# Where the second bias of the edge messages is added, who splits the messages, and what the store and the row loads wait for

## The reference

```python
h = jnp.maximum(_layernorm(x, axis=-1), 0.0)
msg_input = jnp.concatenate([h[src], h[dst]], axis=1)
for t in range(4):
    m = jax.nn.relu(msg_input @ W1[t] + b1[t]) @ W2[t] + b2[t]
    msgs = msgs + jnp.where((edge_type == t)[:, None], m, 0)
agg = jax.ops.segment_sum(msgs, dst, num_segments=num_nodes)
gi = agg @ W_ih.T + b_ih
gh = h @ W_hh.T + b_hh
r = sigmoid(i_r + h_r); z = sigmoid(i_z + h_z); n = tanh(i_n + r * h_n)
out = x + (1 - z) * n + z * h
```

## Time and profile before

| | |
|---|---|
| runs | 1735.42, 1740.06 and 1738.05 us, median 1738.05 us |
| the profiled execution, its own time | 1735.05 us |
| its span in the profile | 1733.2 us |
| mean granted clock of TensorE | 0.978 of the higher level |
| busy: PE, PEld | 1616.9 us (93%), 1421.4 us (82%) |
| busy: DVE, ACT, POOL | 1629.0 us (94%), 1458.7 us (84%), 1003.4 us (58%) |
| chain that ended last, PE's share | PE bank lines 1% each and less, mixed with DVE and ACT lines |

### The profile page before, as it was taken

The page is one execution under the profiler, slowest core; times in us unless marked ns, Lnnn a source line. Parts: engine busy times, 40 slices in busy tenths (PEclk is TensorE's granted clock), DMA queues, the critical chain, the costliest instruction groups (busy, mean ns, idle before and its releaser), DMA issues. The chain is left out here.

```text
span 1733.2 us, 43005 instructions
## 1 busy us (share of the span) xinstructions
PE 1616.9 (93%) x10182; PEld 1421.4 (82%) x10182; DVE 1629.0 (94%) x4752; ACT 1458.7 (84%) x3404; POOL 1003.4 (58%) x1325
## 2 busy tenths in 40 slices
PE   0337999999999999999999999999999999999998
PEld 0326888888888888888888888888888888888887
DVE  8987999999999999999999999999999999999986
ACT  0126999999999999999999999999999999999896
POOL 5755656666666666655555555565655555555500
PEclk9956999999999999999999999999999999999999
DMA  2235777777777777777777777777777777777653
GB/s 84 70 87 154 193 195 206 203 200 200 203 200 203 199 199 203 198 200 196 199 198 200 200 195 201 196 200 195 197 201 194 201 196 199 197 196 200 188 143 100
DMA packets 477080, 320.07 MB, mean 185 GB/s; under 512 B 105917, under 2 KB 463117, under 8 KB 476974
## 3 DMA queue, kind: packets, MB, share of 16 engines
q10 hardware_dynamic: 261792, 156.12, 29.3%
q1 hardware_dynamic: 186638, 107.42, 25.5%
q0 software_dynamic: 28544, 55.41, 13.1%
HBM read 212.08 MB, written 107.07 MB: 184 GB/s over the span
## 5 line engine op out<-in xcount | busy, mean ns | idle before, releaser
L613 POOL DMA_INDIRECT e_x<-in_x,rows_now x816 | 824.4, 1010 | 248.4 <-issue 239.0
L1258 ACT ACTIVATE e_h<-e_x,shift,rstd 128x128 f32<-128x128 f32 x816 | 355.8, 486 | 90.0 <-DVE shift L1114 57.0
L1275 ACT ACTIVATE n_h<-n_x,shift,rstd 128x128 f32<-128x128 f32 x784 | 385.3, 492 | 2.9 <-issue 2.9
L1414 PE MATMUL bank<-n_h_hi,whh_hi 128*128 128x512 f32 x588 | 249.2, 424 | 1.2 <-ACT n_zc L1366 1.2
L1414 PE MATMUL bank<-n_a_hi,wih_hi 128*128 128x512 f32 x588 | 246.4, 419 | 0.9 <-DVE bank L1154 0.9
L1494 PE MATMUL bank<-n_sel,n_win 128*128 128x256 f32 x1568 | 234.7, 292 | 0.4 <-DVE n_sel L1142 0.4
L1416 PE MATMUL bank<-n_a_hi,wih_lo 128*128 128x512 f32 x588 | 232.5, 395 | 0.0
L1416 PE MATMUL bank<-n_h_hi,whh_lo 128*128 128x512 f32 x588 | 231.7, 394 | 0.0
L1415 PE MATMUL bank<-n_h_lo,whh_hi 128*128 128x512 f32 x588 | 231.2, 393 | 0.0
L1142 DVE TENSOR_SCALAR n_sel<-iota,n_rel 128x256 fp32r<-128x256 f32 x784 | 229.6, 357 | 0.1
L1415 PE MATMUL bank<-n_a_lo,wih_hi 128*128 128x512 f32 x588 | 229.6, 391 | 0.0
(11 more groups left out here) (193 smaller groups left out, 3812.4 us busy)
## 6 DMA issues: line engine op xcount, KB each, us to landing
n_win<-messages SPq DMA_DIRECT2D x1568, 64.2 KB
messages<-e_msg ACTq DMA_DIRECT2D x204, 257.0 KB, 2.9
n_x<-in_x ACTq DMA_DIRECT2D x195, 256.0 KB
out<-n_out ACTq DMA_DIRECT2D x195, 256.0 KB
e_x<-in_x,rows_now POOLq DMA_INDIRECT x816
rows_now<-lists SPq DMA_DIRECT2D x204, 2.0 KB
lists<-picks,list_rows POOLq DMA_INDIRECT x54, 2.8
w<-in_W SPq DMA_DIRECT2D x1, 512.0 KB, 5.0
```

The costliest lines, as they stand in the source:

```text
L613: G.indirect_dma_start(e_x[:, s, 2 * end + t, :], None, x, bass.IndirectOffsetOnAxis(ap=rows_now[:, s, t, end:end + 1], axis=0)).then_inc( ...
L1258: last = A.activation(e_h[:, s % 2, k, :], e_x[:, s, k, :], ACT.Relu, scale=rstd[:, slot, col + k:col + k + 1], bias=shift[:, slot, col + ...
L1275: last = A.activation(n_h[:, s % 2, cols], n_x[:, s, cols], ACT.Relu, scale=rstd[:, slot, col + 4 + k:col + 5 + k], bias=shift[:, slot, co ...
L1414: T.matmul(o, w_hi, v_hi, start=start, stop=False, skip_group_check=onto)
```

## The change

1. The bias product on TensorE is gone; the W2 products start the accumulation themselves. b2, spread over all partitions, keeps a tile of its own, b2_two.
2. DVE gets `biased` at the end of its step q + 9: bank BE1 plus b2_two, written as full-precision numbers into the low half's place in e_msg (semaphore e_biased). W1 of the next unit waits for that instead of e_low.
3. e_high copies from there, in SBUF, instead of the bank, in ACT's step q + 10 behind the first pair of normalise_edges and ahead of n_r.
4. `low_half` is gone from DVE; POOL subtracts in SBUF, low = low - high, behind the second pair of gathers and ahead of `write_half`.
5. store_messages stands behind the second pair of normalise_edges; in the head at the end of ACT's step.
6. SP loads the windows by pairs of types. In even steps the loads of types 0 and 1 wait for the store of unit g + 4 and those of types 2 and 3 for unit g + 5; odd steps wait for no store.

```diff
@@ SP, window loads @@
-                    if isinstance(g, int):
-                        for q in range(0 if g == 0 else min(g + AHEAD, UNITS), min(g + AHEAD + 1, UNITS)):
-                            sp.wait_ge(e_stored[q % UNROLL], uses(q, q % UNROLL, UNROLL, 16))
-                    else:
-                        q, qs = g + AHEAD, (m - LAG + 2 + AHEAD) % UNROLL
-                        sp.wait_ge(e_stored[qs], uses(q, qs, UNROLL, 16))
...
+                    for pair_ in range(2):
+                        if m % 2 == 0:
+                            q = g + AHEAD - 1 + pair_
...
+                        for half in range(2):
+                            for t in (2 * pair_, 2 * pair_ + 1):
...
@@ POOL @@
+            def low_half(i, m):
+                q, s = i - 10, (m - 10) % UNROLL
+                if within(q, UNITS):
+                    pool.wait_ge(e_high, q + 1)
+                    G.tensor_tensor(e_msg[:, s, :, D:2 * D], e_msg[:, s, :, D:2 * D].bitcast(F32),
+                                    e_msg[:, s, :, 0:D].bitcast(F32), ALU.subtract).then_inc(e_low, 1)
...
                 if within(i, UNITS):
                     gather(i, m, (1,))
+                low_half(i, m)
                 if h is not None:
                     write_half(h)
@@ DVE @@
-                in_head = isinstance(i, int) and i < LAG - 2
-                if not in_head:
-                    low_half(i, m)
                 ln_part(i, m, 0)
...
+                biased(i, m)
                 if isinstance(i, int) and i == GENERAL_STEP:
                     general_sums()
+
+            def biased(i, m):
+                q, s = i - 9, (m - 9) % UNROLL
+                if within(q, UNITS):
+                    dve.wait_ge(e_messaged, q + 1)
+                    first = 2 * ((m - 9) % 2)
+                    V.tensor_tensor(e_msg[:, s, :, D:2 * D].bitcast(F32),
+                                    bank[BE1][:, message_part].rearrange("p (t d) -> p t d", t=2),
+                                    b2_two[:, first * D:(first + 2) * D].rearrange("p (t d) -> p t d", t=2),
+                                    ALU.add).then_inc(e_biased, 1)
@@ ACT @@
                 normalise_edges(i, m, (0, 1))
+                q, s = i - 10, (m - 10) % UNROLL
+                if within(q, UNITS):
+                    act.wait_ge(e_biased, q + 1)
+                    act.wait_ge(e_tagged, q + 1)
+                    A.activation(e_msg[:, s, :, 0:D], e_msg[:, s, :, D:2 * D].bitcast(F32), ACT.Copy).then_inc(e_high, 1)
...
-                store_messages(i, m)
                 normalise_edges(i, m, (2, 3))
+                in_head = isinstance(i, int) and i < LAG - 2
+                if not in_head:
+                    store_messages(i, m)
@@ PE @@
-                        pe.wait_ge(e_low, q)
+                        pe.wait_ge(e_biased, q)
...
-                    T.matmul(bank[BE1][:, message_part], ones_r[:], b2_rows[:, first * D:(first + 2) * D],
-                             start=True, stop=False)
                     for t in range(2):
                         o = bank[BE1][:, 2 * P + t * D:2 * P + (t + 1) * D]
-                        last = T.matmul(o, e_r[:, s, t * P:(t + 1) * P], w2[:, first + t, :], start=False, stop=t == 1)
+                        last = T.matmul(o, e_r[:, s, t * P:(t + 1) * P], w2[:, first + t, :], start=True, stop=True)
```

More of the change, by code:

```diff
@@ L144, in gnn_layer @@
         b2_rows = sb("b2_rows", [P, TYPES * D], F32R)
+        b2_two = sb("b2_two", [P, TYPES * D])
         row_is = sb("row_is", [P, 2])
@@ L235, in gnn_layer @@
         descends = borrow(n_zc[:], 0, ECOLS)
-        b2_two, b2_hi, b2_lo, b2_parts = (
-            e_msg[:].rearrange("p r t w -> p (r t w)")[:, at * TYPES * D:(at + 1) * TYPES * D] for at in range(4))
-        b2_two, b2_parts = b2_two.bitcast(F32), b2_parts.bitcast(F32)
+        b2_hi, b2_lo, b2_parts = (
+            e_msg[:].rearrange("p r t w -> p (r t w)")[:, at * TYPES * D:(at + 1) * TYPES * D] for at in range(3))
+        b2_parts = b2_parts.bitcast(F32)
         ends = n_d[:].rearrange("p r w -> p (r w)").bitcast(I32).rearrange("p (k e c) -> p k e c", k=SEGMENTS, e=2)
@@ L390, in gnn_layer @@
         e_high = sem("e_high")
+        e_biased = sem("e_biased")
         e_low = sem("e_low")
@@ L557, in step @@
                     if isinstance(g, int) and due(g - 3):
                         sp.wait_ge(n_summed, g - 3)
[L559 to L566, removed]
+                    for pair_ in range(2):
+                        if m % 2 == 0:
+                            q = g + AHEAD - 1 + pair_
+                            if not isinstance(g, int):
+                                qs = (m - LAG + 2 + AHEAD - 1 + pair_) % UNROLL
+                                sp.wait_ge(e_stored[qs], uses(q, qs, UNROLL, 16))
+                            else:
+                                for stored in range(pair_ if g == 0 else q, min(q + 1, UNITS), 2):
+                                    sp.wait_ge(e_stored[stored % UNROLL], uses(stored, stored % UNROLL, UNROLL, 16))
+                        for half in range(2):
+                            for t in (2 * pair_, 2 * pair_ + 1):
+                                at = t % 2 * WIN
+                                if half == 1 and t == 3 and within(g + LAG - 6, UNITS):
+                                    sp.wait_ge(e_tagged, g + LAG - 6)
+                                sp.dma_start(n_win[at:at + WIN, s, 2 * half + t // 2, 0:ROW].bitcast(F32),
+                                             messages[bass.ds(firsts[4 * half + t], WIN), 0:ROW]
+                                             ).then_inc(n_windowed[s], 16)
@@ L1115, in ln_part @@
                                            op0=ALU.mult, op1=ALU.mult).then_inc(ln_shifted, 4)
[L1117 to L1123, removed]
             def step(i, m):
@@ L1174, in step @@
                     last.then_inc(n_stats, 1)
-                if in_head:
-                    low_half(i, m)
                 q, s = i - 4, (m - 4) % UNROLL
@@ L1368, in step @@
                 normalise_nodes(i, m, (3,))
-                q, s = i - 9, (m - 9) % UNROLL
-                if within(q, UNITS):
-                    act.wait_ge(e_messaged, q + 1)
-                    act.wait_ge(e_tagged, q + 1)
-                    A.activation(e_msg[:, s, :, 0:D], bank[BE1][:, message_part].rearrange("p (t d) -> p t d", t=2),
-                                 ACT.Copy).then_inc(e_high, 1)
+                if in_head:
+                    store_messages(i, m)
             pipeline(nc, act, LAST, LOOP_END, step)
```

## The result

The changed kernel took 1826.05 us (median of 4, 1825.17 to 1826.71) against 1736.74 of the kernel before: a ratio of 1.0518, interval 1.0505 to 1.0531. It is slower, as forecast, by 89 us where 58 to 61 were forecast; 1826.05 lies just outside the range that ended at 1826. The profiled execution took 1826.36 us.

What follows compares the result with a forecast made beforehand. It took two hand-overs between TensorE and the others, through n_zc and n_out, to bound the step of 8.002 us. Sum: 1735 + 48 + 16 - 3 = 1796 us; range 1764 to 1826, held at 80%.

Steps and rivals of the forecast that it cites:

- Bias product: On TensorE: its 0.12 us slots lie inside the wait for n_zc, so removing them is worth 0.
- Rival A: TensorE's queue is the bound, so the bias slots' 24 us come straight out, 1711 us; chance 6%.
- `biased` ahead of n_out: On VectorE: n_out starts 0.33 later, delaying gate n's hidden products (HN); +0.25 us a step, +48 us.
- e_high: On ScalarE: the copy from SBUF ahead of n_r fits idle time; cost 0, at most 0.2 us a step.
- low_half on GpSimd: The subtraction ahead of the store takes 0.68 us; cost 0 in a plain step up to 1.5 us.
- VectorE's load stays: On VectorE: `biased` is priced like the low_half it replaces, 0.42 us long, so the load does not change.
- List writes: On GpSimd: the subtraction delays the pick lists' indirect DMAs, making ScalarE late in 13 of 18 steps; +16 us.
- Row loads and store: Store 1.3 us later, loads of odd groups earlier, neither on the path; counted 0.
- Head: At the kernel's start: W1 is freed sooner, but VectorE's work keeps its length; -3 us (-7 to +3).
- the place: `biased` standing ahead of n_out on VectorE, forecast at +0.25 us a step, +48 us.

Runs made afterwards that it cites:

- e4: The kernel before with the bias product left out, so b2 is not added: 1735.44 us, ratio 1.0002.
- e12: The kernel before with TensorE's edge transposes ahead of gate r and the bias product left out: 1730.74 us, ratio 0.9961.
- e2: The changed kernel with GpSimd subtracting 16 instead of 128 columns of each message: 1791.10 us, ratio to the kernel before 1.032.
- e1: The changed kernel with `biased` moved right behind n_out on VectorE: 1853.30 us, ratio to the kernel before 1.068.
- e3: The changed kernel with `biased` behind n_out and GpSimd subtracting 16 of 128 columns: 1770.43 us, ratio to the kernel before 1.0202.
- e7: The kernel before with only the row loads' waits and order and the store's place from the changed kernel: 1735.74 us, ratio 1.0002.
- e5: The changed kernel with the subtraction back on VectorE behind n_out, `biased` staying ahead of it: 1790.51 us, ratio to the kernel before 1.0313.
- e8a: The kernel before with an extra GpSimd subtraction on a scratch tile, waiting for low_half and so starting with n_sel: 1819.36 us, ratio 1.0475.
- e10: The kernel before with only TensorE's edge transposes moved ahead of gate r: 1734.79 us, ratio 1.0002.
- e8b: The kernel before with an extra GpSimd subtraction on a scratch tile, waiting until the step's n_sel is done: 1755.33 us, ratio 1.0109.

## Why the prediction was right in direction and short in size

- *Bias product, 0*: right, shown by e4. Rival A's 24 us would not have come even with both hand-overs loosened (e12: 6).
- *`biased` ahead of n_out, +0.25 a step, +48*: right in size, with the subtraction narrowed: e2 has 0.257 a late step; HN's second product stood 0.39 behind n_out's end, forecast 0.40; the wait rose to 85.1 us in 166 waits.
- *e_high, 0*: nothing speaks against it where the change has it (ScalarE waits 9.6 us for `biased` there, 116 in e1 and e3); no run takes it alone.
- *low_half on GpSimd, "Cost 0 in a plain step, up to a price of 1.5 us"*: this is the step that failed. The price was near, 0.75 for 0.68. But I asked only whether GpSimd would be in time for the store, not what its operation does to VectorE while it runs. It lies beside n_sel, and one n_sel a step takes 0.90 for 0.34, so "VectorE's load stays" did not hold either: n_sel took 92.6 us more. With the subtraction narrowed, 35 us came back, where the sum (1796 against 1735, 61) fell 28 short of the 89 measured; 25 of the 35 are 0.131 a step (8.401 - 8.270) over 194 steps, and the rest lies in the early steps and the head.
- *List writes, +16*: right in kind; ScalarE waited 17 times, 22.7 us. The changed kernel's early steps are 0.166 longer than its late ones, times 66 some 11 us, in which the held-up n_sel has its part.
- *Row loads and store, 0*: right (e7).
- *Head, -3*: wrong in sign. The 190 steps began 4.2 us later. With the subtraction on VectorE the first steps were as early as before (e5: the second group's gate r at 169.5, before 169.7, changed 173.9), so the head's loss comes with GpSimd's part too; why, inside the head, was not taken further.

Put together from these runs: 50 us for the place (194 x 0.257), 25 for n_sel in every step (194 x 0.131), some 11 for the early steps and 4 for the head, 90 of the 91 between the profiled executions. Against the forecast's terms that is 2 more, 25 more, 5 less and 7 more. The division of the first two holds only in this order, since the costs do not add: alone, the subtraction costs 0.355 a step (e8a). That the time lies so close to the range is luck: its upper end, 1826, was reached with dearer list writes (38), and these came out cheaper.

The Trainium skill's "SBUF — State Buffer", section "Who interferes with whom", has the rule that was missing: GpSimd shares a pair of SBUF ports with VectorE, as an exclusive lock for a whole instruction, against VectorE's operations with two SBUF inputs and against those of one input that can run in a two-port mode, tensor_scalar among them. The runs agree: n_sel, a tensor_scalar, and L1085, with two SBUF operands, are held up (0.90 for 0.34; 0.71 to 1.20 for 0.18, 17 times in the changed kernel), while n_out, n_ted and the statistics are not. That n_sel is held up until the subtraction is over was measured; that it is the lock that does it is the page's explanation. One row stays open: L1083, which reads one SBUF tile as both its operands, overlaps the subtraction 76 times in the changed kernel, begun some 0.02 us ahead of it, and keeps its 0.19, where n_sel begun as shortly ahead are held up.

The Trainium skill's "GPSIMD Engine Reference", section 4.1, would have priced the subtraction at twice VectorE's time, 0.84 from 0.42, an estimate; measured 0.75. Its advice to keep two-input work on VectorE came true here for another reason than the price.

## What to carry to other kernels

Before work moves to an engine with free time, look at what its neighbour does in that very stretch: GpSimd had 40% of its time free, and an operation of 0.75 us on it made VectorE's n_sel 0.47 us a group longer (92.6 us over 196). What such a delay costs hangs on the neighbour's idle time: 0.13 a step where another wait had made room for it (e2 against the changed kernel), 0.355 where there was little (e8a). So price two changes together, not as a sum. Ask of an instruction that is put ahead of another not what it costs but who waits for the one behind it, and of one that is put later, who waits for it (e1 missed that). And a product that stands inside a wait is free to keep: taking it away returns nothing until what ends the wait is moved.

## What the runs showed that was not expected

- Two bounds seem to lie within 0.1 us of each other: the hand-overs and VectorE's own load both give 8.0 us a step (before, e10, e12).
- A subtraction whose result nobody reads slowed the kernel by 4.8% at one place (e8a), and by 1.1% some 1.1 us later in the step (e8b).
- GpSimd's own instruction is stretched less than VectorE's: 0.81 mean beside n_sel, 0.74 behind it.
